# Border between layers 2 and 3 of a graph network kernel rearranged, and the degree count's one-hots laid out by twos

## The reference

```python
src = jnp.concatenate([src, arange(6250)]); dst = jnp.concatenate([dst, arange(6250)])
deg = segment_sum(ones, dst)
dinv = where(deg > 0, rsqrt(deg), 0)
norm_edge = dinv[src] * dinv[dst]
h = x                                  # 6250 x 256
for W, b in ((W1, b1), (W2, b2), (W3, b3)):      # 256x512, 512x512, 512x256
    h = relu(segment_sum((h @ W)[src] * norm_edge[:, None], dst) + b)
out = layernorm(x + h)                 # no scale, no shift, eps 1e-5
```

## Time and profile before

| engine | busy us | share of the span |
|---|---|---|
| TensorE matmuls | 2190.7 | 91% |
| TensorE weight loads (beside them) | 1466.1 | 61% |
| VectorE | 872.1 | 36% |
| ScalarE | 733.4 | 31% |
| GpSimd | 1704.3 | 71% |

### The profile page before, as it was taken

One profiled execution on the slowest core, in us unless ns is written; L12 is line 12 of the kernel. 1 busy time (PEld: TensorE's weight loads), 2 busy tenths in 40 slices (PEclk: granted clock), 3 DMA queues, 4 the chain that ended last, 5 costly groups with the idle time before them and its releaser, 6 DMA issues.

```text
span 2397.1 us, 33266 instructions
## 1 busy us (share of the span) xinstructions
PE 2190.7 (91%) x10765; PEld 1466.1 (61%) x10765; DVE 872.1 (36%) x1212; ACT 733.4 (31%) x1550; POOL 1704.3 (71%) x1768
## 2 busy tenths in 40 slices
PE   6977889999999998999999999999898889999998
PEld 6955567777777774444444444444444378888886
DVE  8888322222222212232333323433232233434333
ACT  6701223333333311232332323223231134343333
POOL 5167777777777775777777777777777767776774
PEclk8789989999999999999999999999999999999999
DMA  7335767767766766888888888888888777778884
GB/s 223 122 111 180 230 200 209 209 209 210 209 209 209 209 200 185 253 257 254 263 255 250 256 263 256 250 254 261 261 262 267 212 232 227 227 229 267 283 276 131
DMA packets 232394, 543.61 MB, mean 227 GB/s; under 512 B 39228, under 2 KB 107699, under 8 KB 232259
## 3 DMA queue, kind: packets, MB, share of 16 engines
q0 software_dynamic: 122592, 387.10, 54.5%
q1 hardware_dynamic: 91011, 121.92, 14.8%
q10 hardware_dynamic: 18656, 32.75, 4.3%
HBM read 455.62 MB, written 86.00 MB: 226 GB/s over the span
## 4 chain that ended last, share of the span: by engine, by line
PE 55%; POOL 17%; issue 15%; DMA 8%; DVE 3%; POOLq 1%; ACT 1%; ACTq 0%; DVEq 0%; SPq 0%
POOL rows L775 17%; PE ps_acc L1744 7%; PE ps_h L1839 7%; PE ps_o L1800 6%; DMA rows<-table,idx 6%; PE ps_d L1744 6%; PE ps_acc L1740 5%; PE ps_d L1850 5%; PE ps_T L1839 5%; PE ps_h L1789 2%; PE ps_d L1689 2%; PE ps_acc L1736 2%; PE ps_d L1736 2%; DMA rows<-table_parts,idx 1%; PE ps_e L1821 1%
## 5 line engine op out<-in xcount | busy, mean ns | idle before, releaser
L775 POOL DMA_INDIRECT rows<-table,idx x1081 | 1047.7, 969 | 390.2 <-issue 306.4
L1744 PE MATMUL ps_acc<-rows,sel 128*128 128x512 f32 (+2 forms) x1122 | 492.0, 566 | 87.4 <-DMA rows<-table,idx 66.0
L775 POOL DMA_INDIRECT rows<-table_parts,idx x483 | 457.6, 947 | 149.7 <-issue 137.8
L993 DVE SCALAR_TENSOR_TENSOR sel<-ps_e,firsts,dstT 128x1152 f32<-128x1152 f32 (+1 forms) x194 | 274.2, 1413 | 621.4 <-PE ps_acc L1744 213.5
L1744 PE MATMUL ps_d<-rows,sel 128*128 128x512 f32 (+1 forms) x850 | 411.3, 607 | 38.6 <-DMA rows<-table,idx 38.0
L1744 PEld LDWEIGHTS ps_acc<-rows,sel 128*128 128x128 f32 x1122 | 205.0, 200 | 239.7 <-issue 151.3
L1800 PE MATMUL ps_o<-low,hT 128*128 128x512 f32 (+1 forms) x784 | 271.9, 490 | 1.0 <-ACT hT L1427 1.0
L1740 PE MATMUL ps_acc<-rows,sel 128*128 128x256 bf16 (+1 forms) x1533 | 243.4, 275 | 23.1 <-DMA rows<-table_parts,idx 13.5
L1744 PEld LDWEIGHTS ps_d<-rows,sel 128*128 128x128 f32 x850 | 147.3, 191 | 176.0 <-issue 122.3
L1850 PE MATMUL ps_d<-big 128*128 128x256 bf16 x1470 | 227.1, 273 | 4.1 <-issue 3.5
L1839 PE MATMUL ps_T<-pairs_r,rows_r 128*128 128x512 f32 x686 | 213.4, 427 | 12.0 <-ACT rows_r L1518 8.0
(11 more groups left out here) (214 smaller groups left out, 2161.7 us busy)
## 6 DMA issues: line engine op xcount, KB each, us to landing
rows<-table,idx POOLq DMA_INDIRECT x1081, 4.3
table<-made SPq DMA_DIRECT2D x49, 256.0 KB
acc<-table SPq DMA_DIRECT2D x49, 256.0 KB
table_pairs<-made_r SPq DMA_DIRECT2D x49, 256.0 KB, 4.2
built<-big SPq DMA_DIRECT2D x30, 384.0 KB, 3.9
low<-built ACTq DMA_DIRECT2D x30, 384.0 KB, 5.0
built_bytes<-big SPq DMA_DIRECT2D x54, 192.0 KB, 4.9
low<-built_bytes ACTq DMA_DIRECT2D x54, 192.0 KB, 3.7
```

The costliest lines, as they stand in the source:

```text
L775: pool.indirect_dma_start(out=to, out_offset=None, in_=its[0:nodes, :], in_offset=bass.IndirectOffsetOnAxis(ap=idx[:, of, k:k + 1], axis=0 ...
L993: v.scalar_tensor_tensor(to[:, k:k + FRONT, :], numbers.unsqueeze(1).broadcast_to([P, FRONT, P]), firsts[:, bass.ds(t, 1)], dstT[:, bass.d ...
L1744: return mm(to[:, 0:w], sel[:, k, :], rows_of[phase][:, k, 0:w] if first is None else first, start=start, stop=stop)
```

## The change

It has three parts.

1. *Degree count.* `SIDE` goes from 4 to 2, so that one column's values lie 4 bytes apart, and `steps` moves from SBUF to the PSUM bank `ps_h` (made in SBUF, then copied).
2. *SP.* The last turn of the loop is written out: the own row of tile 48 is loaded without the wait for `slots_used` (`late=False`), and tile 47 is stored right behind it.
3. *Border on TensorE and ScalarE.* Slots 0, 1, 2 of the first window of layer 3 come in front of `turn` of tile 48, slots 3 and 4 between `turn` and `product`; the 21 dense matmuls that stood in front of and between slots 0 to 5 now stand together behind the product, in front of slot 5 (`AHEAD`). On ScalarE the first two `widen` stand between the relus and `make` of tile 48, and the loads of dense tile 1 come behind that.

```diff
-SIDE = 4
+SIDE = 2
+AHEAD = 5
-        steps = sel[:, :, :].rearrange("p a b -> p (a b)")[:, 0:HALVES * SIDE // 2].bitcast(BF16).rearrange(
-            "p (j c) -> p j c", j=HALVES)
+        steps_made = sel[:, :, :].rearrange("p a b -> p (a b)")[:, 0:HALVES * SIDE // 2]
...
+        steps_kept = ps_h[:, 0:HALVES * SIDE // 2]
+        steps = steps_kept.bitcast(BF16).rearrange("p (j c) -> p j c", j=HALVES)
...
-            v.tensor_copy(steps[:, :, :], steps_f[:, 0:HALVES].unsqueeze(2).broadcast_to([P, HALVES, SIDE])).then_inc(steps_done, 1)
+            step(v.tensor_copy(steps_made.bitcast(BF16).rearrange("p (j c) -> p j c", j=HALVES),
+                               steps_f[:, 0:HALVES].unsqueeze(2).broadcast_to([P, HALVES, SIDE])))
+            v.tensor_copy(steps_kept, steps_made).then_inc(steps_done, 1)
...
-                        with sp.Fori(ROUND * ROUNDS + 3, T) as t:
+                        with sp.Fori(ROUND * ROUNDS + 3, T - 1) as t:
                             rows_and_store(t, nth(1, t - 1))
+                        own_rows(T - 1, late=False)
+                        store(T - 2, nth(1, T - 2))
                         store(T - 1, nth(1, T - 1))
...
+                if between is not None:
+                    between()
                 make(phase, t, s, per)
...
+                def first_pieces():
+                    for x in range(2):
+                        widen(0, x)
                 for t in range(ROUND * ROUNDS, T):
-                    tile(1, t, nth_of_windows(1, t), nth(1, t), 1)
+                    tile(1, t, nth_of_windows(1, t), nth(1, t), 1, between=first_pieces if t == T - 1 else None)
...
-                widen(0, 0)
...
-                        for at in range(u * DENSE_OF * T // n, (u + 1) * DENSE_OF * T // n):
+                        if first and u < AHEAD:
+                            its = range(0)
+                        else:
+                            its = range(0 if first and u == AHEAD else u * DENSE_OF * T // n, (u + 1) * DENSE_OF * T // n)
+                        for at in its:
...
+                        slots(phase, n, ORDER[:AHEAD - 2], first, None, beside, ps, True, phase + 3)
+                        turn(1, nth(1, T - 1))
+                        slots(phase, n, ORDER[AHEAD - 2:AHEAD], None, None, beside, ps, True)
+                        product(1, nth(1, T - 1), T - 1)
+                        slots(phase, n, ORDER[AHEAD:-1], None, None, beside, ps, True, None, late_landed)
...
-                turn(1, nth(1, T - 1))
-                product(1, nth(1, T - 1), T - 1)
```

More of the change, by code:

```diff
@@ L1457, in make, with tile @@
                     nc.scalar.activation(made_r[:, 0:C], ps_o[:, 0:C], ACT.Copy, scale=dinv[:, t:t + 1]).then_inc(high_made, 1)
-            def tile(phase, t, n, s, per, built_half=None):
+            def tile(phase, t, n, s, per, built_half=None, between=None):
                 scale(phase, t, n, s, per)
@@ L1621, in group @@
                         deviation(of_gather(g - 1, 2))
-                    pieces(1)
                     if not first:
+                        pieces(1)
                         deviation(of_dense(g - 1, 3))
@@ L1906, in first_window @@
                     ps = ps_sums[n % 2]
-                    slots(phase, n, ORDER[:-1], rows_of[phase][:, 0, 0:WIDTH[phase]], None, beside, ps, phase == 2, phase + 3, late_landed_in(n))
+                    late_landed = late_landed_in(n)
+                    first = rows_of[phase][:, 0, 0:WIDTH[phase]]
+                    if phase == 1:
+                        slots(phase, n, ORDER[:-1], first, None, beside, ps, False, phase + 3, late_landed)
+                    else:
+                        slots(phase, n, ORDER[:AHEAD - 2], first, None, beside, ps, True, phase + 3)
[3 more added lines that the diff above has]
+                        slots(phase, n, ORDER[AHEAD:-1], None, None, beside, ps, True, None, late_landed)
                     if phase == 1:
```

## The result

| kernel | median, us | against the kernel before |
|---|---|---|
| before (4 runs) | 2390.5 | |
| changed (4 runs) | 2373.28 | 0.9927 [0.9912, 0.9942] |

The kernel is 17.2 us faster; 2370.5 was forecast. The profiled execution took 2371.75 us, its span is 2369.9 us.

What follows compares the result with a forecast made beforehand. The prediction took layer 3 to be bound by TensorE and the start by the degree-count chain; 10.7 us from the count plus 9.2 from the border made 19.9, so 2390.4 - 19.9 = 2370.5 us, range 2364 to 2382.

Steps and rivals of the forecast that it cites:

- The stall: Degree count: VectorE's 6.35 us compare beside GpSimd's stops waiting once one input is in PSUM; 5.1 us gained, 0 if not.
- VectorE's own pass: Degree count: VectorE's compare by twos with numbers in PSUM stays at its present 1.23 us.
- the rival on the slow side: Degree count: VectorE's compare from PSUM by twos loses its double rate and becomes the limit; 2436 us, chance 0.03.
- TensorE's pitch: Degree count: VectorE's columns by twos cost what contiguous ones do, 0.06 us each instead of 0.09; pass 2.2 us, not 3.1.
- The rival by the Trainium skill's lines of 16 bytes: Degree count: 8 bytes apart already gets full rate, so the pitch stays and only the stall goes; 2376.1 us, chance 0.2.
- What is late next: Degree count: ScalarE's 2.89 us passes, then VectorE's last work, set the end; degrees taken at 84.0 instead of 94.72 us.
- GpSimd's wait for the pair: Border: SP issues tile 47's pair sooner, GpSimd's 4.33 us wait goes; it goes on at 1910.96, 4.0 us sooner.
- The turn stays at 1920.95: Border, TensorE: slots 0 to 2 fit into the wait for ScalarE's scaling, so the turn keeps its time and costs nothing.
- Slots 3 to 5: landing is just in time: Border: their rows land by about 1921.4; TensorE takes slots 3 and 4 at 1921.6, 0.5 us, beside ScalarE's relus.
- The product is at the full clock, because the gap shrinks: Border, TensorE: the gap before the turn shrinks from 1.62 to about 0.7 us; tile 48's product takes 1.9 us, not 3.45.
- The border, 9.2 us: Layer 2 to 3: TensorE reaches slot 5 at 1929.4 instead of 1938.63; bounds about 4 to 9.2 us.
- `make` behind two widenings: Border, ScalarE: make waits until about 1927.0 instead of 1925.7, tile 48's rows and pairs stored some 1.3 us later, hidden.

Runs made afterwards that it cites:

- PSUM alone: The kernel before with only the degree count's steps copied to PSUM, columns still by fours (8 bytes apart): 2386.28 us, 0.9982.
- the twos alone: The kernel before with only SIDE changed from 4 to 2, steps left in SBUF: 2386.53 us, 0.9985.
- SP's part alone: The kernel before with only SP's last loop turn written out, tile 48's own row loaded without the wait for slots: 2393.48 us, 0.999.
- the last version: The changed kernel with tile 48's product moved in front of slots 3 and 4: 2370.31 us (0.9914), then 2375.76 us (0.9911).
- the border with SP: The kernel before with the TensorE and ScalarE border order and SP's change, degree count as before: 2390.41 us, 0.9971.

## Why the prediction was right, point by point

- **The stall, 5.1 us.** Right. PSUM alone takes the degrees 5.2 us sooner, and the compare went from 6.35 to 1.23 us beside the same GpSimd instruction. The Trainium skill's rule on two SBUF inputs (SBUF — State Buffer, "Who interferes with whom") holds in both halves here: 6.57 us with two (the twos alone), 1.23 us with one (the changed kernel).
- **VectorE's own pass.** Right: 1.23 us by twos out of PSUM, no loss of rate; the rival on the slow side is refuted.
- **TensorE's pitch.** Right in kind, and of the right size or better: 207 ns by twos, and the 32 matmuls of a pass take 1.65 us, about 0.05 us each where 0.06 was taken from four loads. The difference cost nothing, because ScalarE and VectorE set the pass. The rival by the Trainium skill's lines of 16 bytes (SBUF — State Buffer, "Door 1: The DMA port swizzle") is refuted for TensorE's operands: by fours, two values in each 16 bytes, they took 269 ns in every trace that has them, by twos 207.
- **What is late next.** Right. Passes come every 2.89 us, VectorE's small work follows, the degrees are taken at 83.68 us against 84.0 forecast (83.0 to 83.7 in six traces). The count was put at 10.7 us and gave 11.2 by the traces, 12.5 [9.3, 15.8] by the times.
- **GpSimd's wait for the pair.** Right: 4.33 us became 0.44 (0.3 to 0.5 us in six of the seven traces with SP's new order, 1.6 in one). In places of the kernel before (plus 15.53, the advance of product 47) GpSimd goes on at 1909.99; 1910.96 was forecast.
- **"The turn stays at 1920.95".** Wrong. It starts at 1901.61, which is 1917.14 in those places, 3.8 us sooner. I had moved SP's stores and asked only who waits for them, not whose transfers they stand among: layer 2's last 8 matmuls now wait 0.32 us for their rows instead of 2.56, and ran at the full clock, 3.70 us instead of 5.40. The kernel with SP's part alone shows that the wait goes with SP's order. The clock is another matter: those 8 matmuls took 3.70 us in two of the six traces with the old order too.
- **"Slots 3 to 5: landing is just in time".** About right in time and wrong in what it meant: slots 3 and 4 are taken at 1920.0 in those places (1921.6 forecast), but since the turn was sooner, TensorE stood 2.21 us for them with the product behind. It is the wait that the last version takes out.
- **"The product is at the full clock, because the gap shrinks".** Failed as a reason. In three traces of the changed kernel the product took 1.89, 3.26 and 3.57 us; in the kernel before 3.45 and 1.97. The clock there is given by something that these traces don't show.
- **The border, 9.2 us.** Against the trace it was worked out from the gain was 11.5 us (37.42 - 25.89). Over five traces of the old TensorE and SP order (mean 34.8) and four of the new (the three of the changed kernel and the border with SP, mean 27.2) it is 7.6 us, and the times give 6.9 [4.3, 9.3]. The term was mis-sized: it took a half clock of the profiled execution, worth up to 3.5 us (37.4 against 33.9 for one kernel), as the kernel's own. The warning stood in the numbers: that execution was 8.4 us above the median, and it was set against the median without asking which piece was dear.
- **`make` behind two widenings.** Wrong in direction: tile 48's pair was to be stored 1.3 us later and is issued at 1909.13, which is 1924.66 in those places against 1927.49 before, since all that leads to it was sooner. That nothing of this reaches TensorE was right: slot 5 to the end took what it took before.
- **The sum.** 19.9 us forecast, 17.2, 18.7 and 17.8 us by the medians of the three groups, 17.5 to 19.6 by the ratios. A count a little too small and a border too large. That the border's part came so near is partly luck: the turn 3.8 us sooner and the new wait of 2.21 us were both not foreseen, and they work against each other.

Left open: what makes the middle 1800.5 to 1811.9 us from one execution to the next, and what sets the clock at the border. The six traces with the new count have 1804.4 us in the mean there, the five with the old one 1806.0, which such a spread does not tell apart. A small part of the spread lies right behind the count: its small matmuls and what follows them on TensorE, up to the next turning of rows, took 12.5 to 14.9 us, and both ends were seen with the old count.

## What to carry to other kernels

Work out a local change from the trace, but ask first which stretches of that one execution were at the lower clock; a gain that only returns the clock is not the edit's, and a second trace of the same kernel is the cheapest test there is. Where GpSimd and VectorE work side by side, put one input of VectorE's elementwise instruction in PSUM: a copy of 98 words took out a stall of 5 us. Move an instruction ahead of another only when its own input comes sooner too: TensorE's and ScalarE's new order brought nothing that could be measured while GpSimd still waited for SP to store tile 47's pair. And of a transfer that is moved, ask whose rows it was travelling among.

## What the runs showed of the hardware

- TensorE's bf16 operands 8 bytes apart cost 269 ns for 98 columns, 4 bytes apart 207, as contiguous ones (204 to 207).
- VectorE's second SBUF input delays GpSimd as well: its compare took 6.13 us in all seven traces in which VectorE's compares had one SBUF input, and 6.48 to 7.94 in the six with two. Its gather issues beside them took 945 to 949 ns at the median against 1184 to 1398.
- For one kernel and the same waits, tile 48's product ran at 1.2 GHz in one execution and at 2.4 GHz in another. So did the small matmuls behind the count: before, the first 14 took 3.07 us in one trace and 1.72 in the other, with a mean granted clock of 0.73 and 1.00 in the 2 us behind the taking of the degrees.
